# A graph network kernel: PE's loop over the blocks holds 24 blocks per turn instead of 8

## What is computed

```python
src = incidence[1]
dst = incidence[0]
h = node_embedding
for _ in range(DEPTH):        # DEPTH = 3
    msgs = jnp.take(h, src, axis=0)
    msgs = jax.nn.relu(msgs @ W_edge + b_edge)
    agg = jax.ops.segment_sum(msgs, dst, num_segments=N_NODES)
    h = jax.nn.relu(jnp.concatenate([agg, h], axis=-1) @ W_agg + b_agg)
...
x = _layernorm(x + h)
```

## Time and profile before

| | us |
|---|---|
| median of 3 runs | 4232.28 |
| lowest and highest | 4230.75, 4237.94 |
| the profiled execution, its own time | 4241.99 |
| its span, from the first to the last instruction | 4239.9 |

### The profile page before, as it was taken

How to read it: one execution, slowest core, us unless ns; L and a number is a source line. 1 busy time by engine, 2 the same in 40 slices (tenths; PEclk the granted TensorE clock), 3 DMA queues, 4 the chain that set the end, 5 groups by cost and what they waited for, 6 DMA issues and landing times. The chain is left out here.

```text
span 4239.9 us, 101860 instructions
## 1 busy us (share of the span) xinstructions
PE 3694.8 (87%) x19862; PEld 2419.0 (57%) x19863; DVE 3215.7 (76%) x11131; ACT 2264.4 (53%) x4904; POOL 2890.5 (68%) x2867
## 2 busy tenths in 40 slices
PE   5777759999989999799999688888888769999998
PEld 3555548888778877577776344444444334444443
DVE  6888856666656766677777478888888659999998
ACT  1333325555545555465555345444454358777776
POOL 3777757776377766477663677777777377777775
PEclk8999979999999999999999899999999889999999
DMA  2555547887678877588776455555555334444443
GB/s 83 180 174 174 171 141 240 245 238 239 194 214 241 247 228 227 175 255 258 243 248 197 143 154 153 160 155 157 159 154 160 92 103 128 129 129 129 129 130 95
DMA packets 583445, 749.61 MB, mean 177 GB/s; under 512 B 146825, under 2 KB 407664, under 8 KB 583276
## 3 DMA queue, kind: packets, MB, share of 16 engines
q1 hardware_dynamic: 476652, 554.66, 40.3%
q0 software_dynamic: 106624, 193.25, 18.2%
HBM read 426.02 MB, written 321.54 MB: 176 GB/s over the span
## 5 line engine op out<-in xcount | busy, mean ns | idle before, releaser
L797 POOL DMA_INDIRECT mp_gathered<-msg_rows,other_idx x784 | 754.7, 963 | 355.2 <-issue 197.0
L1112 POOL DMA_INDIRECT ll_gathered<-msg_rows,other_idx x392 | 373.1, 952 | 221.9 <-issue 115.2
L815 PE MATMUL bank<-mp_edge_hot,mp_gathered 128*128 128x256 bf16 x3528 | 476.2, 275 | 37.2 <-POOLq L785 19.2
L559 POOL DMA_INDIRECT by_window<-so_pay,so_pos_i x392 | 387.8, 989 | 166.3 <-issue 111.8
L1698 POOL DMA_INDIRECT ff_agg<-at_rows,last_idx x392 | 382.9, 977 | 116.2 <-issue 106.9
L1403 POOL DMA_INDIRECT at_of_dst<-x_rows,node_idx x392 | 377.7, 964 | 119.4 <-issue 119.4
L1399 POOL DMA_INDIRECT at_of_src<-x_rows,kv_idx x392 | 371.9, 949 | 119.3 <-issue 97.4
L871 ACT ACTIVATE mp_h_out<-bank,mp_b_agg 128x256 f32<-128x256 f32 x392 | 185.6, 473 | 483.4 <-PE bank L833 475.7
L815 PEld LDWEIGHTS bank<-mp_edge_hot,mp_gathered 128*128 x3528 | 346.6, 98 | 107.3 <-issue 64.5
L904 DVE TENSOR_SCALAR mp_edge_hot<-digits,mp_first_col,column 128x256 bf16<-128x256 bf16 x1176 | 339.7, 357 | 69.3 <-issue 56.7
L1810 PE MATMUL bank<-ff_h_cols,ff_w 128*128 128x512 f32 x784 | 370.1, 594 | 0.9 <-ACT ff_h_cols L1843 0.9
(11 more groups left out here) (261 smaller groups left out, 8984.7 us busy)
## 6 DMA issues: line engine op xcount, KB each, us to landing
msg_rows<-mp_msg_out SPq DMA_DIRECT2D x392, 192.0 KB
mp_h_in<-h_cols SPq DMA_DIRECT2D x392, 128.0 KB
h_cols<-mp_h_out SPq DMA_DIRECT2D x392, 128.0 KB
msg_rows<-so_msg_out SPq DMA_DIRECT2D x98, 384.0 KB
h_cols<-so_h_out SPq DMA_DIRECT2D x98, 256.0 KB
ll_h_in<-h_cols SPq DMA_DIRECT2D x196, 128.0 KB
x_rows<-ll_x SPq DMA_DIRECT2D x98, 256.0 KB
skip_rows<-ll_skip SPq DMA_DIRECT2D x98, 256.0 KB
```

The source lines that it names most:

```text
L559: pool.indirect_dma_start(core.by_window, bass.IndirectOffsetOnAxis(ap=pos_i[k][:, t:t + 1], axis=0), pay[k][:, t, :], None, bounds_check= ...
L797: pool.indirect_dma_start(gathered[:, r * PARTS * D:(r + 1) * PARTS * D], None, core.msg_rows[layer % 2], bass.IndirectOffsetOnAxis(ap=cor ...
L815: product = nc.tensor.matmul(agg_bank[k], gathered[:, bass.ds(at + d * D, D)], hot, start=(first and d == 0), stop=True, skip_group_check= ...
L1112: pool.indirect_dma_start(gathered[:, r * PARTS * D:(r + 1) * PARTS * D], None, core.msg_rows[(LAYERS - 1) % 2], bass.IndirectOffsetOnAxis ...
```

## The change

PE alone gets another helper, `long_blocks`, in both stages. DVE and ACT keep `blocks` with 8 blocks per turn. In message passing PE writes out blocks 0 to 7, then 7 turns of 24 blocks (8 to 175), then the rest from 176. In the last layer it writes out 0 to 15, then 7 turns of 24 (16 to 183), then the rest from 184. Semaphores, counts and the work of a block are the same.

```diff
+LONG = 24
...
+        def long_blocks(eng, turn):
+
+            def straight(n):
+                def do(lag, step):
+                    if 0 <= n + lag < NW:
+                        step(n + lag, (n + lag) % MSGS, (n + lag) // MSGS)
+                turn(do)
+            for n in range(MSGS):
+                straight(n)
+            rounds = (NW - MSGS) // LONG
+            with aligned(eng, 0, rounds) as i:
+                for r in range(LONG):
+                    turn(lambda lag, step: step(LONG * i + (MSGS + r + lag), (r + lag) % MSGS, LONG // MSGS * i + (MSGS + r + lag) // MSGS))
+            for n in range(MSGS + rounds * LONG, NW + 5):
+                straight(n)
+
...
-                    blocks(pe, turn, MSGS)
+                    long_blocks(pe, turn)
...
+        def long_blocks(eng, turn):
...
+            for n in range(2 * TURN):
+                straight(n)
+            rounds = (NW - 2 * TURN) // LONG
+            with aligned(eng, 0, rounds) as i:
+                for r in range(LONG):
+                    turn(lambda lag, step: step(LONG * i + (2 * TURN + r + lag), (r + lag) % TURN, LONG // TURN * i + (2 * TURN + r + lag) // TURN))
+            for n in range(2 * TURN + rounds * LONG, NW + 2 * TURN):
+                straight(n)
+
...
-            blocks(pe, turn)
+            long_blocks(pe, turn)
```

More of the change, by code:

```diff
@@ L1026, in blocks, with straight, do @@
                 straight(n)
+        def long_blocks(eng, turn):
+            def straight(n):
+                def do(lag, step):
+                    if 0 <= n + lag < NW:
+                        step(n + lag, (n + lag) % TURN, (n + lag) // TURN)
+                turn(do)
+            for n in range(2 * TURN):
[6 more added lines that the diff above has]
+                straight(n)
         def group(step):
```

## The result

| | median us (lowest to highest, runs) | profiled execution, its span |
|---|---|---|
| before | 4232.81 (4230.75 to 4237.94, 4) | 4241.99, 4239.9 |
| after | 4335.44 (4332.00 to 4342.20, 4) | 4342.20, 4340.3 |

The change makes the kernel slower: the ratio is 1.0244, 95% interval 1.0231 to 1.0257, or 103 us. The forecast was 4283, and its upper end was 4321. The sign and its cause were right, the size was half of what came.

The account below looks back on a forecast made before the run. The prediction took PE's own stream to bound the kernel. Removing 47 branches back (-21 us) and adding 18 waits for re-read code (+72) gave +51 us on a median of 4232.3, so 4283 us, range 4208 to 4321.

Parts of the forecast that it names:

- The sign and its cause: Whole kernel: slower by 51 us, because PE's long loop bodies are read again at branches back; slower was given 0.72.
- PE is the bound: Message passing and last layer: PE's own stream sets the time, so what it gains or loses arrives in the span.
- Nothing is read again before, and the long bodies are: PE's loops: bodies of 2.6 instruction blocks stay, those of 7.8 and 8.05 are re-read each turn; over 200 q8 packets.
- three times what the trace shows to stay, and it touches one block more by reading ahead: PE's new loop bodies: the reason given for choosing the far end, not resident, with 72 us added.
- The rival that split the bodies at eight blocks: PE's loops: bodies of 2007 instructions stay, the last layer's 2060 doesn't; +3 us, 4235 us, chance 0.08.
- Number and price of the waits: PE's branches back: 18 waits for re-read code, 4.2 us each, 4.0 above a resident branch, 72 us added.
- What is removed: PE's turn ends: 65 branches back become 18, so 47 removed at 0.45 us each, 21 us saved.
- three ways of pricing it: One PE branch back: branch alone 0.218 us, message passing's loop exit 0.42, last layer's exit 0.47; 0.45 taken.
- Reading again while PE works: Inside PE's long bodies: blocks behind the re-read first one are read while PE works, at no cost.
- The rival with this cost: Inside PE's long bodies: each re-read instruction block costs 1 us more, +144 us, 4430 us, chance 0.04.
- Blocks written out straight: Outside PE's loops: 40 more blocks written out, at most 4 us, put at nothing.
- at most 0.1 us is left of each: First block written out behind the loop: 2.61 us against 2.51, so at most 0.1 us for each of 40 blocks.

Follow-up runs that it names:

- pad7: long16 plus never-run products in a skipped place (13 in message passing, 11 in the last layer), bodies of 6.8 to 6.9 blocks: 4234.9 us, ratio 1.0002.
- pad8: As pad7, but with 21 and 19 never-run products, bodies of 7.8 to 7.9 blocks: 4419.4 us, ratio 1.0441.
- hint24: The changed kernel (24 blocks per turn) with a hint at the top of the loop body announcing the branch back: 4248.3 us, ratio 1.0034.
- long16: The changed kernel with turns of 16 blocks instead of 24 (LONG = 16): 4229.5 us, ratio 0.9991 to the kernel before.
- straight_all: The kernel before with all PE blocks of message passing and the last layer written out, no loop over blocks: 4213.8 us, ratio 0.9947.

## Why the prediction missed the size

**PE is the bound.** Right. POOL waits for PE more than before, PE for POOL less, and nearly every microsecond that PE lost is in the span (98.7 of 100.4).

**Nothing is read again before, and the long bodies are.** Right. Forecast: over 200 packets; came 221. The step "three times what the trace shows to stay, and it touches one block more by reading ahead" was argued from a limit that no row showed. pad7, pad8 and hint24 show it now. The Trainium skill ("Runtime: NRT & Kernel Launch", Instruction fetch mechanics) has PE's instruction memory at 128 KiB in blocks of 16 KiB, or eight blocks, and pad7 (61 packets) and pad8 (339) agree; the block that is read past the loop's end and takes one of the eight is not in that rule, and it is what decided here. What the section says of taken branches goes by a window of two pages, which the prediction left out, and there the measurement differs: bodies of 2.6 to 6.9 blocks are branched back through in 0.21 to 0.22 us. The last layer's body is 2060 instructions by my count, 8.05 blocks, and with the hint it stayed too, with no q8 packet in 420 us. The count is probably a dozen too high: a body that reaches into a ninth block, with the block behind it, would read ten packets in a turn, and the last layer's turns read nine, as those of message passing do. The rival that split the bodies at eight blocks fell anyway: the ones of 2007 went as well.

**Number and price of the waits.** 18, as forecast. The price was taken as 4.2 us from an estimate of 3.9 to 5.0; it came as 4.56, so 18 x 4.34 = 78 in place of 18 x 4.0 = 72. Its three parts came out as estimated: over the 18 the packet starts 2.0 us behind the branch (1.3 to 2.7), takes 1.2, and the branch ends 1.4 behind it, where the working had 1.7, 0.93 to 1.96 and 1.3. Most of the shortfall is that I took 4.2 and not the middle of these, leaning on the one wait in the trace of before (3.3 us), whose packet starts with the branch. This term is 6 us short.

**The clock behind a wait.** Not in the sum. The three steps behind each wait lose 0.52 us together, 9 us in 18 places. Between 600 and 2450 us the granted clock is at its lower level for 92 us before and 181 after, and the runs with stops tie at least 0.3 to 0.5 us of such a place to it; that the rest is the sequencer catching up is not shown. The step with the branch itself loses 4.38, the wait and next to nothing else: the slow products are in it too (2.10 us), but the load of words was short there (0.595 to 0.611 us behind all 12 waits of message passing, where the earlier trace rows has 1.162 and the loads of before run from 0.59 to 1.43). This term was 9 us, from nothing.

**What is removed.** 0.45 us per branch was too much. The other eighth steps win 0.36 us each, so 47 x 0.36 = 17 in place of 21 (0.25 to 0.31 each in long16, hint24 and pad7, by the same reckoning, so 12 to 15). Of the three ways of pricing it, two compared a turn's end with a loop's exit, one pair of blocks each, and pairs inside a turn differ by as much as the difference that I read from them. Term short by 4 us.

**Reading again while PE works.** This is the step that failed. I wrote that the blocks behind the first "are read while PE works", and put that at nothing, on the ground that a block of instructions lasts PE some 8 us and is read in 2. It cost 27.1 us: 0.07 for each of 387 ordinary steps (0.08 to 0.09 in message passing, 0.04 in the last layer). Over 155 packets that were read again it is 0.17 us each. In long16, where nothing is read again, the same kind of step loses nothing, and in hint24, with the same body as here, it loses 9.7 us in 387, about what the hint itself costs. The ground was right for the array and wrong for the sequencer. Where PE's sequencer comes into a block that has just been read, two of its own register instructions stand 210 to 320 ns apart where 97 to 124 is usual, and a skip branch that lands there takes up to 364 ns (the row of L743 above; 229 before). Between 720 and 1080 us I count some 25 such gaps in the changed kernel, 12 in the one before, none with the hint. The turn of the last layer that read only two packets (2006.8 to 2079.5 us) is the nearest thing to a control inside the kernel itself: it has one such gap where the other six turns of that loop have four to eight, and its 21 ordinary steps lose nothing (-0.3 us) where those of the other five turns behind a branch back lose 1.2 to 2.3. PE's own sums show the pace, six steps inside one turn, none with a load of words, in the changed kernel and then the same six before:

```profile
802.60 1.15 PE L832 MATMUL bank<-mp_edge_hot,mp_gathered 128*128 128x256 bf16 x9
...
818.11 1.15 PE L832 MATMUL bank<-mp_edge_hot,mp_gathered 128*128 128x256 bf16 x9
...
794.35 1.15 PE L815 MATMUL bank<-mp_edge_hot,mp_gathered 128*128 128x256 bf16 x9
...
809.43 1.15 PE L815 MATMUL bank<-mp_edge_hot,mp_gathered 128*128 128x256 bf16 x9
```

That is 15.51 us, 2.585 per block of nodes, and it was 15.08, or 2.51. The rival with this cost (1 us per block of instructions, 4430) had the place right and the size six times too large; I gave it 0.04 and left it out of the range, when a small form of it belonged into the sum. straight_all shows such a loss where nothing is read twice, some 0.15 us per block read, with the same long skip branches. So it isn't only a matter of branches back: it is the price of meeting code newly read, which a loop that stays doesn't pay. pad8 pays more of it, 0.145 us per ordinary step of message passing with nine packets in 16 steps, where the changed kernel pays 0.085 with nine in 24. Per packet, reckoned as in straight_all, that is 0.26 and 0.23 us; why it is more than 0.15 there is open.

**The sum, corrected:** -17 + 78 + 9 + 27 = +97. The steps of the profiled executions give +99, their spans +100, and the medians +103; the last few us are not placed. The four terms are read from those same steps, so that they add up is no further proof; the proof of each is in the runs above.

**Blocks written out straight.** Put at nothing, and right for the 40 blocks here: the steps outside the loops show no difference. The step "at most 0.1 us is left of each" was the loss that came inside the body, and I dropped it as too small to tell; times 387 it isn't.

## What to carry to other kernels

Before unrolling a hardware loop, count the body's instructions as the engine reads them (weights and product apart, f32 products twice, skipped code too) and look at the engine's instruction queue in the profile: if it is silent during the loop, the body stays. On PE here it stayed up to 6.9 blocks of 256 with one block ahead; past that every branch back cost some 5 us at once, and 1.5 us more spread over a turn of 24 blocks (27.1 / 18). If branches back are worth removing, write out the whole loop rather than a longer turn, and allow some 0.15 us for each block of code that is then read (message passing; in the last layer the loss didn't show).

## What the runs showed of the hardware

- On PE a taken branch to a block of instructions that is no longer there takes 3.8 to 5.2 us, mean 4.56 (18 in the changed kernel), and 3.5 to 5.8, mean 4.23 (30 in pad8); a taken one to a block that is there 0.21 to 0.22, one that is not taken 0.08 to 0.09.
- A loop's body has to fit in eight blocks of 256 instructions together with one more, by all signs the block behind the loop's end: 6.9 blocks stay and 7.9 don't, and then nine are read in a turn (47 of the 48 turns behind a branch back in the changed kernel and pad8; in one only two were). With a hint on the back edge 7.9 stay and 8.4 don't.
- Code that never runs is read and counts like any other: 8 products more in a skipped place, 16 times in a body, cost 184.5 us.
- The hint costs 0.9 us per turn (28 us in 33 turns), though its instruction takes 31 to 55 ns.
- A newly read block costs PE some 0.15 us (written out straight) to 0.23 (long loop) in message passing; two register instructions of its sequencer stand 210 to 320 ns apart there where 97 to 124 is usual.
- PE standing for 4 to 5 us comes back at 1.2 GHz, with or without reading, and the lower level lasts 3.4 to 10 us in the record; by keeping it at work in the stop, 0.3 to 0.5 us per stop were won in message passing.
